# A pose, text, state-space and sparse-attention model on one core: a 42-node operand and two queues in the set-up, and attention units taken in pairs from a copy of the logits in SBUF

## The chip, the core and the metric

The kernel runs on one core of a Trainium2 chip. It is one program for five engines (TensorE or PE, VectorE or DVE, ScalarE or ACT, GpSimd or POOL, SyncE or SP) that meet only through semaphores. The metric is the device time of one execution in microseconds (us); lower is better.

## The reference

Four sequences of 128 frames of 50 joints with 3 coordinates, and four token sequences of 512, are turned into `[4, 640, 128]`. Cut to what matters here:

```python
def _gat(x, src, dst, W, a_s, a_d, bias):          # x [512 frames, 50 joints, channels]
    h = (x @ W).reshape(G, Jn, H, C)               # 4 heads, 148 edges
    es = einsum('gjhc,hc->gjh', h, a_s)[:, src];  ed = einsum('gjhc,hc->gjh', h, a_d)[:, dst]
    ...                                            # softmax over the edges into dst, weighted sum
for W, a_s, a_d, bg, R, g, b in layers:            # channels 3 -> 64 -> 128 -> 64
    x = gelu(layer_norm(_gat(x, ...) + x @ R, g, b))
frames = layer_norm(x.reshape(512, 50 * 64) @ fpW + fpb)
h = concat(frames, conv of one-hot tokens)         # a sum of three gathered rows per token
h = h + state_space_stage(layer_norm(h))           # four layers, 640 steps
x = layer_norm(h);  x = x + depthwise_conv3(x) + pos_b
q, k, v = x @ qkv_w.T + qkv_b                      # 8 heads of 16 channels
idx = top_k(q @ k.T, 16)                           # per query row, 640 keys
h = h + (softmax over those 16 of q @ k.T * scale, times v) @ wo_w.T + wo_b
```

## The kernel before, in words

Three stages follow each other, each a block of its own with a program for each engine: `embed_stage` (0 to about 1350 us), `mamba_stage` (to about 5400 us, untouched by the change) and `ffn_stage` (to the end).

**Embed.** SP issues 5 loads of the token ids once POOL has cleared their tile (`cleared`), then 33 loads of edges and weights with one semaphore, `loaded`, then the frames' coordinates `x0T`, 3 rows by 12800. POOL gathers the token rows by 48 indirect loads. DVE waits for all of `loaded`, then ranks the 148 edges by target (L440 to L456; PE sorts them with one-hot matrices), builds edge masks, and forms for each of the three layers the eight score columns of the weight operand `wc[l]` (L480, L481: weights times `as`, `ad`, summed over a head). `set_dve` (L491) says that this is done. Then come two passes `pb` over pairs of batches. Each pass has three attention layers and the projection of the frames. A layer begins with a projection (`project`, L405): for each of 100 nodes (50 joints of two batches) a matmul with the node's 128 frames as stationary operand and `wc[l]` as moving operand, 136 columns wide in layer 0 (64 of W, 64 of R, 8 scores), with 3 rows in layer 0. Two nodes make a group G (`NG` is 50), ACT copies the first 64 columns of a group to `hbuf` (L321), DVE takes the rest (L529, L531). Then follow edge scores, softmax scans and the products over edges. Buffers `accA` and `accB` take the layers' sums in turn; `x0T` lies in `accB`, so the coordinates of pass 1 are loaded after the last normalisation of pass 0 (`nrm_ready`).

**Attention (`ffn_stage`).** A loop of four batches. A batch has a preparation (L1554 to `vp`: sum, layer norm, transposition, convolution, q, k, v, each step on another engine than the one before) and 40 units c: 5 tiles t of 128 query rows by 8 heads hd. A unit passes through the engines like this:

- PE `logits`: 128x640 of q k into PSUM, `LG[:, k, :]`, k = c % 2 (L1498)
- DVE: the largest 8 of each row (`top1`, L1616), replaced by -3e38 in `cut1` (L1621), the next 8 (`top2`, L1624), replaced in `cut2` (L1629). All four are over 640 elements, each needs the one before; the first two read `LG`
- POOL: `negm`, minus the maximum (L1416)
- ACT: `e_all`, exp of `LG` plus `negm` (L1461), and `e_cut`, exp of `cut2` plus `negm` (L1445)
- POOL `sub`: `prob` is `e_all` minus `e_cut`, which leaves the 16 largest (L1407)
- PE: 5 transposes into `PT` (L1507); ACT: copy to `probT` (L1438); PE: 5 products with `vp`, summed into `Ov` (L1516)
- once in 8 units DVE's `finish_a` (row sums, division), PE's and ACT's output projection of the tile, `finish_b` (residual), SP's store

The order on each engine is written out by hand in one loop over c: in turn c PE does `logits(c+1)`, `transposes(c-2)`, `pv(c-3)`; ACT `exp_cut(c-1)`, `e_all` of c, `probT_copy(c-2)`; POOL `negm` of c, `sub(c-1)`; DVE the four searches of c. `LG` has two halves; `logits(c+1)` waits until unit c-1 has been through both `cut1_ready` and `exp_ready`. The batches are a hardware loop (`Fori`), so a batch's preparation stands behind all of the units of the batch before on every engine.

## Time and profile before

| | us |
|---|---|
| median of 3 runs | 6161.43 |
| range of the runs | 6158.26 to 6162.38 |
| the profiled execution | 6194.43 |
| its span in the trace | 6192.4 |
| busy in the span: DVE, POOL, PE, ACT | 5546.6 (90%), 4510.6 (73%), 3863.3 (62%), 3290.5 (53%) |

The page of the profile is one execution; it took 33 us longer than the median run, and 2.0 us more than its own span. The page's chain of work that ended last is followed back through the last stage only; it names DVE for 7% of the span, issue for 3%, PE for 2%. Its costliest groups of instructions, led by `m_hs` on POOL (2990.4 us) and DVE (2964.0 us), belong to the untouched stage. For the stages of the change the timeline and the windows are read instead. In a window's row the busy times stand in the order PE, PE's weight loads, DVE, ACT, POOL, then PE's granted clock (1.00 is 2.4 GHz, 0.50 is 1.2 GHz), the DMA engines' busy share and GB/s.

### The profile page before, as it was taken

What the parts mean: (1) busy time and instruction counts of PE and PEld (TensorE: products, weight loads), DVE (VectorE), ACT (ScalarE), POOL (GpSimd) and SP (SyncE); (2) the same over time, 40 slices, a digit from 0 to 9 for tenths busy, and PEclk for the clock granted to TensorE, in tenths of its full rate; (3) what the DMA queues carried; (4) which work ended last, traced back from release to release, by engine and by line L of the source; (5) the groups of instructions that cost most, each with busy time, mean ns of one, the idle gap of its engine ahead of it and who ended that gap; (6) DMA issues with size and microseconds to landing.
All of it is one profiled execution on the core that took longest, in us unless ns stands there. A gap on an engine that the chain in (4) does not pass through costs nothing. (4 is left out here: it accounts for less than half of the span.)

```text
span 6192.4 us, 60179 instructions
## 1 busy us (share of the span) xinstructions
PE 3863.3 (62%) x13720; PEld 2225.0 (36%) x13720; DVE 5546.6 (90%) x7803; ACT 3290.5 (53%) x5742; POOL 4510.6 (73%) x3041
## 2 busy tenths in 40 slices
PE   3402432237767677677676776766767766577767
PEld 3202421123334333333333333433333333265556
DVE  3798678839999999999999999999999999787778
ACT  1302232226666666666666666666666665554445
POOL 3303210329999999999999999999999999633334
PEclk9756576659999999999999999999999999888788
DMA  1000000024444444444444444444444444200000
GB/s 28 1 11 1 2 1 11 1 90 173 170 170 168 171 168 170 168 172 169 169 170 168 168 172 169 168 169 168 170 169 171 166 168 169 100 2 2 2 2 2
DMA packets 171471, 694.85 MB, mean 112 GB/s; under 512 B 27969, under 2 KB 34626, under 8 KB 171138
## 3 DMA queue, kind: packets, MB, share of 16 engines
q1 hardware_dynamic: 169608, 688.25, 30.7%
q0 software_dynamic: 1536, 3.14, 0.2%
q14 instruction: 233, 1.91, 0.1%
q8 instruction: 94, 1.54, 0.1%
HBM read 684.77 MB, written 6.55 MB: 112 GB/s over the span
## 5 line engine op out<-in xcount | busy, mean ns | idle before, releaser
L851 POOL TENSOR_TENSOR m_hs<-m_u,m_BC 128x1280 f32<-128x1280 f32 x1024 | 2990.4, 2920 | 76.5 <-DVE m_u L1232 76.5
L1198 DVE TENSOR_TENSOR_SCAN m_hs<-m_PS,m_hs 128x640 f32<-128x640 f32 x2048 | 2964.0, 1476 | 12.6 <-ACT m_PS L908 6.7
L1082 PE MATMUL m_PS<-m_pr,ident 128*128 128x512 f32 (+1 forms) x6144 | 2443.4, 534 | 846.5 <-DVE m_pr L1206 846.1
L1082 PEld LDWEIGHTS m_PS<-m_pr,ident 128*128 128x128 f32 x6144 | 1110.8, 191 | 2079.0 <-DVE m_pr L1206 1077.6
L908 ACT ACTIVATE m_PS<-m_dt,m_A 128x640 f32<-128x640 f32 x2048 | 1612.4, 793 | 430.5 <-DVE m_hs L1198 404.4
L858 POOL TENSOR_TENSOR m_pr<-m_hs,m_BC 128x384 f32<-128x384 f32 x1024 | 1047.5, 1023 | 95.2 <-DVE m_hs L1198 93.4
L1206 DVE TENSOR_TENSOR m_pr<-m_hs,m_PS 128x896 f32<-128x896 f32 x1024 | 1087.4, 1062 | 7.2 <-DVE m_hs L1198 6.9
L292 POOL TENSOR_TENSOR g_prod<-g_hbuf,g_E 128x128 f32<-128x128 f32 x592 | 246.1, 452 | 862.8 <-ACT g_E L344 845.6
L897 ACT COPY m_PS<-m_BC 128x448 f32<-128x448 f32 x1024 | 548.2, 535 | 427.0 <-DVE m_u L1232 83.1
L1416 POOL TENSOR_SCALAR f_negm<-f_top 128x1 f32<-128x1 f32 x160 | 33.5, 209 | 449.4 <-DVE f_top L1616 278.0
L378 PE MATMUL g_TB<-ident,g_nrm 128*128 128x128 f32 x200 | 64.3, 323 | 440.2 <-DVE g_nrm L517 429.2
L1498 PE MATMUL f_LG<-f_kT,f_qh 128*128 128x128 f32 (+1 forms) x640 | 242.2, 508 | 132.4 <-ACT f_e_all L1461 127.3
L346 ACT ACTIVATE g_rstd<-g_rstd 128x100 f32<-128x100 f32 x6 | 1.7, 286 | 582.0 <-DVE g_rstd L621 582.0
L600 DVE TENSOR_TENSOR g_accA<-g_accA,g_prod 128x128 f32 x592 | 223.4, 377 | 52.5 <-issue 23.0
L1407 POOL TENSOR_TENSOR f_prob<-f_e_all,f_e_cut 128x640 f32<-128x640 f32 x160 | 246.4, 1540 | 8.4 <-ACT f_e_cut L1445 8.4
L376 PE MATMUL g_TB<-ident,g_nrm 128*128 128x128 f32 x200 | 45.6, 314 | 321.6 <-DVE g_nrm L517 321.0
L1461 ACT ACTIVATE f_e_all<-f_LG,f_negm 128x640 f32<-128x640 f32 x160 | 126.9, 793 | 173.7 <-DVE f_cut L1621 173.7
L1516 PEld LDWEIGHTS f_O<-f_vp,f_probT 128*128 128x128 f32 x1600 | 218.6, 215 | 0.0
L1516 PE MATMUL f_O<-f_vp,f_probT 128*128 128x17 f32 x1600 | 214.7, 272 | 0.0
L1498 PEld LDWEIGHTS f_LG<-f_kT,f_qh 128*128 128x128 f32 x640 | 122.8, 214 | 239.0 <-issue 123.4
L1120 PE MATMUL m_PS<-m_xT,m_convw 128*128 128x160 f32 x1024 | 179.6, 319 | 43.7 <-DVE m_pr L1206 39.8
L378 PEld LDWEIGHTS g_TB<-ident,g_nrm 128*128 128x128 f32 x200 | 29.3, 147 | 482.4 <-DVE g_nrm L517 270.4
(246 smaller groups left out, 4486.6 us busy)
## 6 DMA issues: line engine op xcount, KB each, us to landing
m_BC<-m_scr SPq DMA_DIRECT2D x1024, 640.0 KB, 3.7
m_scr<-m_CB SPq DMA_DIRECT2D x32, 160.0 KB, 4.3
m_hs<-in_cwr SPq DMA_DIRECT2D x4, 512.0 KB, 3.9
out<-f_res SPq DMA_DIRECT2D x20, 64.0 KB, 1.6
m_inw<-in_in_w SPq DMA_DIRECT2D x4, 256.0 KB, 3.9
m_dtw<-in_dw SPq DMA_DIRECT2D x4, 256.0 KB, 3.6
m_xw<-in_xw SPq DMA_DIRECT2D x8, 64.0 KB, 3.7
m_outw<-in_ow SPq DMA_DIRECT2D x4, 128.0 KB, 3.4
```

The source lines that it names most:

```text
L292: ins = pool.tensor_tensor(slots[:, e % SLOTS[l]].rearrange("p b (h c) -> p b h c", c=C), hb[l][:, :, bass.ds(j, 1), :].rearrange("p b o ( ...
L600: ins = v.tensor_tensor(to, to, slots[:, e % SLOTS[l]], ALU.add)
L851: pool.tensor_tensor(hs[:, g % RH], u[:, p % 2], BC[:, g % UB:g % UB + 1, 0:S].to_broadcast([P, DT, S]), ALU.mult).then_inc(w_ready, 1)
L858: pool.tensor_tensor(pr[:, g % RP, :].rearrange("p (d t) -> p d t", d=DT)[:, :, XD:S], hs[:, g % RH, :, XD:S], BC[:, g % UB:g % UB + 1, S ...
L897: act.copy(C[:, 0:XD], BC[:, g % UB, S:S + XD]).then_inc(c_ready, 1)
L908: act.activation(half[d], dt_[:, p % 2, d], ACT.Exp, scale=A[:, l, d, n:n + 1]).then_inc(da_ready, 1)
L1082: ins = pe.matmul(Y[:, a:e], ident[:], pr[:, g % RP, a:e], start=False, stop=False, skip_group_check=True)
L1198: v.tensor_tensor_scan(hs[:, g % RH, d, :], half[d], hs[:, g % RH, d, :], 0.0, ALU.mult, ALU.add).then_inc(scan_done, 1)
L1206: v.tensor_tensor(pr[:, g % RP, :].rearrange("p (d t) -> p d t", d=DT)[:, :, 0:XD], hs[:, g % RH, :, 0:XD], C[:, 0:XD].unsqueeze(1).to_bro ...
L1407: pool.tensor_tensor(prob[:, k, :], e_all[:, k, :], e_cut[:, k, :], ALU.subtract).then_inc(prob_ready, 1)
L1498: ins = pe.matmul(LG[:, k, a:e], qh[:, hd, t * P:(t + 1) * P], kT[:, a:e], start=True, stop=True)
L1516: ins = pe.matmul(Ov[:, hd, :], probT[:, k, j, :], vp[:, j, hd, :], start=(j == 0), stop=(j == TILES - 1))
```

## The change

**Set-up.** SP issues the 3 edge loads first, before the wait for `cleared`, and behind them 8 loads for layer 0; then the ids and the coordinates. The other 26 loads are issued by ACT. POOL makes its index tiles before it clears. DVE starts the ranking at `edges_loaded`; then come the score columns of layer 0, a mask and the ids (`ids_ready`, on which the gathers wait), then the sorting steps; the score columns of layers 1 and 2 come last, behind `loaded`.

**42-node operand.** In layer 0 the stationary operand is `x0C`, 126 rows: 3 coordinates by 42 nodes, in two overlapping windows (nodes 0 to 41 and 8 to 49). The moving operand is `block0`, 126 rows by 42 blocks of 136 columns, zero but for the rows of the block's own node. ACT makes the 42 blocks (`blocks()`, one activation of 126x136 each, scaled by a column of `mask`) once in the set-up and once more in layer 2 of pass 0. One matmul of 272 columns does a group. Both lie in `accB`; six loads instead of one bring the coordinates, those of pass 1 now after the normalisation in front of layer 2.

**Attention in pairs.** The four batches are written out. A slot n handles units 2n and 2n+1. ACT copies each unit's logits to `lcopy` in SBUF, four deep; the searches and `e_all` read that copy, and `logits` waits for `lcopied` alone. DVE does each of the four steps for both units before the next step. The preparation of batch b+1 (`prepare`, four steps on DVE and PE, three on ACT) stands in slots 20 to 23 of batch b, when the searches are over and PE and ACT still have units to finish.

The core of the diff (the rest are buffer indices, semaphores and the same steps put into functions):

```diff
+wc = [sb(f"wc{l}", [(CROW, P, P)[l], 2 * COUT[l] + 2 * H]) for l in range(3)]
...
-x0T = accB[0:3].rearrange("p (b j) c -> p b j c", b=2)
+N0 = 2 * COUT[0] + 2 * H
+accB_f = accB[0:CROW].rearrange("p j c -> p (j c)")
+block0 = accB_f[:, 0:CH * N0].rearrange("p (j n) -> p j n", n=N0)
+x0C = accB_f[:, CH * N0:CH * N0 + 4 * P].rearrange("p (b k c) -> p b k c", b=2, k=2)
+mask = sb("mask", [CROW, CH])
...
+        for dst, at in ((ei_row[:], T["edges"].unsqueeze(0).to_broadcast([P, 2, NE])),
+                        (ei_col[:, 0, :], T["edgesT"][0:E1, :]), (ei_col[0:E2, 1, :], T["edgesT"][E1:NE, :])):
+            sp.dma_start(dst, at).then_inc(edges_loaded, 16)
+        for dst, at in loads_first():
+            sp.dma_start(dst, at).then_inc(first_loaded, 16)
...
-                sp.wait_ge(nrm_ready, pb * (3 * NG))
-            sp.dma_start(x0T, T["xT"][:, bass.ds(pb * 2, 2)]).then_inc(x_loaded, 16)
+                sp.wait_ge(nrm_ready, (pb * 3 - 1) * NG)
+            for k in range(2):
+                for c in range(3):
+                    sp.dma_start(x0C[CH * c:CH * c + CH, :, k, :],
+                                 T["xT"][c, pb * 2:pb * 2 + 2, CAT[k]:CAT[k] + CH, :].rearrange("b j p -> j b p")
+                                 ).then_inc(x_loaded, 16)
...
+        rest = loads_rest()
+        assert len(rest) == N_REST, len(rest)
+        for dst, at in rest:
+            act.dma_start(dst, at).then_inc(loaded, 16)
+        act.wait_ge(wc0_ready, 1)
+        def blocks():
+            for j in range(CH):
+                act.activation(block0[:, j, :], wc[0][:], ACT.Copy, scale=mask[:, j:j + 1]).then_inc(block_ready, 1)
+        blocks()
+        act.wait_ge(loaded, N_REST * 16)
...
+                if l == 2 and pb + 1 < PB:
+                    act.wait_ge(nrm_ready, (pb * 3 + 2) * NG)
+                    blocks()
...
+                    if l == 0:
+                        k = 0 if 2 * g < CH else 1
+                        at = 2 * g - CAT[k]
+                        pe.matmul(banks(l, G).rearrange("p a n -> p (a n)"), x0C[:, bb, k, :],
+                                  block0[:, at:at + 2, :].rearrange("p a n -> p (a n)"),
+                                  start=True, stop=True).then_inc(proj_ready, 1)
+                        return
...
+        v.wait_ge(edges_loaded, 3 * 16)
         v.wait_ge(iota_ready, 4)
...
+        v.wait_ge(first_loaded, N_FIRST * 16)
+        scores(0, CROW)
+        chain(v.tensor_tensor(mask[:], ident[0:CROW, 0:CH], ident[0:CROW, CH:2 * CH], ALU.add))
+        chain(v.tensor_tensor(mask[:], mask[:], ident[0:CROW, 2 * CH:3 * CH], ALU.add))
+        v.sem_inc(wc0_ready, 1)
+        v.wait_ge(ids_loaded, 5 * 16)
...
+    PAIRS = UNITS // 2
+    PER = HEADS // 2
+    LONG = PAIRS + 5
...
+lcopy = sb("lcopy", [P, 4, S])
...
+            for n in range(PAIRS + 1):
+                if n < PAIRS:
+                    negate(2 * n)
+                    negate(2 * n + 1)
+                if n >= 1:
+                    sub(2 * n - 2)
+                    sub(2 * n - 1)
...
+            def copy_logits(c):
+                act.wait_ge(logits_ready, b * UNITS + (c + 1))
+                if c >= 4:
+                    act.wait_ge(cut1_ready, b * UNITS + (c - 3))
+                    act.wait_ge(exp_ready, b * UNITS + (c - 3))
+                act.copy(lcopy[:, c % 4, :], LG[:, c % 2, 0:S]).then_inc(lcopied, 1)
+            def exp_all(c):
+                act.wait_ge(neg_ready, b * UNITS + (c + 1))
+                if c >= 4:
+                    act.wait_ge(prob_ready, b * UNITS + (c - 3))
+                act.activation(e_all[:, c % 4, :], lcopy[:, c % 4, :], ACT.Exp, bias=negm[:, c % 4:c % 4 + 1]
...
+                for q in range(2):
+                    if 2 <= n < PAIRS + 2:
+                        probT_copy(2 * (n - 2) + q)
+                    if n < PAIRS:
+                        exp_all(2 * n + q)
+                if n + 1 < PAIRS:
+                    copy_logits(2 * n + 2)
+                    copy_logits(2 * n + 3)
+                if n < PAIRS:
+                    exp_cut(2 * n)
+                    exp_cut(2 * n + 1)
+                if b + 1 < B and 0 <= n - PAIRS < 3:
+                    prepare(b + 1, n - PAIRS)
...
-                    pe.wait_ge(cut1_ready, b * UNITS + (c - 1))
-                    pe.wait_ge(exp_ready, b * UNITS + (c - 1))
+                    pe.wait_ge(lcopied, b * UNITS + (c - 1))
...
+            for n in range(LONG):
+                if n >= PER + 3 and (n - PER - 3) % PER == 0:
+                    o_out((n - PER - 3) // PER, 1)
+                old = 2 * (n - 2)
+                if 2 <= n < PAIRS + 2:
+                    transposes(old)
+                    transposes(old + 1)
+                    pv(old)
+                if n + 1 < PAIRS:
+                    logits(2 * n + 2)
+                    logits(2 * n + 3)
+                if 2 <= n < PAIRS + 2:
+                    pv(old + 1)
+                if n >= PER + 2 and (n - PER - 2) % PER == 0:
+                    o_out((n - PER - 2) // PER, 0)
+                if b + 1 < B and 0 <= n - PAIRS < 4:
+                    prepare(b + 1, n - PAIRS)
...
+                two = (2 * n, 2 * n + 1) if n < PAIRS else ()
+                for c in two:
+                    v.wait_ge(lcopied, g0 + (c + 1))
+                    if c >= 4:
+                        v.wait_ge(neg_ready, g0 + (c - 3))
+                    apart(v)
+                    v.max(top1[:, c % 4, :], lcopy[:, c % 4, :]).then_inc(top_ready, 1)
+                if n >= PER + 2 and (n - PER - 2) % PER == 0:
+                    finish_a((n - PER - 2) // PER)
+                if n >= PER + 4 and (n - PER - 4) % PER == 0:
+                    finish_b((n - PER - 4) // PER)
+                for c in two:
+                    v.wait_ge(top_ready, g0 + (c + 1))
                     if c >= 2:
-                        v.wait_ge(neg_ready, g0 + (c - 1))
+                        v.wait_ge(cut2_ready, g0 + (c - 1))
                     apart(v)
-                    v.max(top1[:, k, :], LG[:, k, 0:S]).then_inc(top_ready, 1)
-                    v.wait_ge(top_ready, g0 + (c + 1))
-                    if c >= 1:
-                        v.wait_ge(cut2_ready, g0 + c)
-                    apart(v)
-                    v.match_replace(cut1[:], top1[:, k, :], LG[:, k, 0:S], CUT).then_inc(cut1_ready, 1)
+                    v.match_replace(cut1[:, c % 2, :], top1[:, c % 4, :], lcopy[:, c % 4, :], CUT).then_inc(cut1_ready, 1)
+                for c in two:
                     v.wait_ge(cut1_ready, g0 + (c + 1))
                     apart(v)
-                    v.max(top2[:, k, :], cut1[:]).then_inc(top2_ready, 1)
+                    v.max(top2[:, c % 2, :], cut1[:, c % 2, :]).then_inc(top2_ready, 1)
+                for c in two:
                     v.wait_ge(top2_ready, g0 + (c + 1))
                     if c >= 2:
                         v.wait_ge(expcut_ready, g0 + (c - 1))
                     apart(v)
-                    v.match_replace(cut2[:, k, :], top2[:, k, :], cut1[:], CUT).then_inc(cut2_ready, 1)
-                if c >= HEADS + 2 and (c - HEADS - 2) % HEADS == 0:
-                    finish_a((c - HEADS - 2) // HEADS)
-                if c >= HEADS + 4 and (c - HEADS - 4) % HEADS == 0:
-                    finish_b((c - HEADS - 4) // HEADS)
+                    v.match_replace(cut2[:, c % 2, :], top2[:, c % 2, :], cut1[:, c % 2, :], CUT).then_inc(cut2_ready, 1)
+                if b + 1 < B and 0 <= n - PAIRS < 4:
+                    prepare(b + 1, n - PAIRS)
```

ACT in the steady stretch, before: one unit to a turn (`f_` names the stage; `e_cut`, `e_all` and the copy to `probT`).

```order
L1438 COPY f_probT<-f_PT 128x640 [waits f_pv_done,f_probT_ready]
L1445 ACTIVATE f_e_cut<-f_cut,f_negm 128x640 [waits f_prob_ready,f_cut2_ready]
L1457 REGISTER_ALU
L1461 ACTIVATE f_e_all<-f_LG,f_negm 128x640 [waits f_prob_ready,f_cut1_ready,f_neg_ready]
L1438 COPY f_probT<-f_PT 128x640 [waits f_pv_done,f_probT_ready]
L1445 ACTIVATE f_e_cut<-f_cut,f_negm 128x640 [waits f_prob_ready,f_cut2_ready]
L1457 REGISTER_ALU
```

The same place now: the copies of the logits are new, and everything comes twice (two rows of `probT` and `e_all` alternate).

```order
L1530 COPY f_lcopy<-f_LG 128x640 [waits f_exp_ready,f_cut1_ready,f_logits_ready] x2
L1522 ACTIVATE f_e_cut<-f_cut,f_negm 128x640 [waits f_prob_ready,f_cut2_ready] x2
L1515 COPY f_probT<-f_PT 128x640 [waits f_pv_done,f_probT_ready]
L1536 ACTIVATE f_e_all<-f_lcopy,f_negm 128x640 [waits f_prob_ready,f_neg_ready]
L1515 COPY f_probT<-f_PT 128x640 [waits f_pv_done,f_probT_ready]
L1536 ACTIVATE f_e_all<-f_lcopy,f_negm 128x640 [waits f_prob_ready,f_neg_ready]
L1530 COPY f_lcopy<-f_LG 128x640 [waits f_exp_ready,f_cut1_ready,f_logits_ready] x2
```

`e_all` no longer waits for `cut1_ready`, and a unit's copy of the logits stands ahead of the `e_cut` of the pair before.

PE in the same stretch, before, one turn:

```order
L1498 MATMUL f_LG<-f_kT,f_qh 128x512 [waits f_exp_ready,f_cut1_ready]
L1498 MATMUL f_LG<-f_kT,f_qh 128x128
L1507 MATMUL f_PT<-ident,f_prob 128x128 [waits f_probT_copied,f_prob_ready]
L1507 MATMUL f_PT<-ident,f_prob 128x128 x4
L1516 MATMUL f_O<-f_vp,f_probT 128x17 [waits f_probT_copied]
L1516 MATMUL f_O<-f_vp,f_probT 128x17 x4
```

Now, one slot (transposes of two units, one PV, logits of two units, the other PV):

```order
L1610 MATMUL f_PT<-ident,f_prob 128x128 [waits f_probT_copied,f_prob_ready]
L1610 MATMUL f_PT<-ident,f_prob 128x128 x4
L1610 MATMUL f_PT<-ident,f_prob 128x128 [waits f_probT_copied,f_prob_ready]
L1610 MATMUL f_PT<-ident,f_prob 128x128 x4
L1619 MATMUL f_O<-f_vp,f_probT 128x17 [waits f_probT_copied]
L1619 MATMUL f_O<-f_vp,f_probT 128x17 x4
L1599 MATMUL f_LG<-f_kT,f_qh 128x512 [waits f_lcopied]
L1599 MATMUL f_LG<-f_kT,f_qh 128x128
L1599 MATMUL f_LG<-f_kT,f_qh 128x512 [waits f_lcopied]
L1599 MATMUL f_LG<-f_kT,f_qh 128x128
L1619 MATMUL f_O<-f_vp,f_probT 128x17 [waits f_probT_copied]
L1619 MATMUL f_O<-f_vp,f_probT 128x17 x4
```

The logits come behind the transposes and a PV whose waits are on `prob` and `probT`, and wait for ACT's copy instead of DVE and the exponential.

SP's queue at the start, now (before, the ids came first and `g_accB<-in_xT` behind all 38 others):

```order
L268 DMA g_E<-in_edges 128x296
L268 DMA g_ei_col<-in_edgesT 128x2
L268 DMA g_ei_col<-in_edgesT 20x2
L270 DMA g_wc<-in_W 42x64
...
L270 DMA g_M<-in_ad 128x64
L272 DMA g_ids<-in_ids 128x16
...
L276 DMA g_ids<-in_ids 1x4x3
L282 DMA g_accB<-in_xT 42x2x128 x6
L286 DMA g_hbuf<-in_fpW 128x25x128
L282 DMA g_accB<-in_xT 42x2x128 x6
```

The edges lead, the coordinates follow the ids, and the second set waits for `g_nrm_ready` of an earlier layer.

## Rows read from the trace of the kernel before

**Rows 1.** windows: from:to length, then busy us (x instructions) of PE, PEld, DVE, ACT, POOL; clock.

```profile
5420.00:6192.00 772.00, 572.86 (x3182) 454.96 (x3180) 600.51 (x1134) 372.65 (x517) 278.21 (x323) 0.84 0.01 2
```

**Rows 2.** timeline of the set-up: start us, us, engine, line, operation, [idle before it].

```profile
9.91 0.45 SPq L248 DMA_DIRECT2D g_E<-in_edges  x1
11.07 0.17 DVE L436 TENSOR_SCALAR g_ids<-g_ids 128x16 int32<-128x16 int32 x1 [11.07 <-DMA g_ids<-in_ids]
...
30.06 0.24 DVE L440 CAST g_F<-g_E 128x148 f32<-128x148 int32 x1 [18.74 <-DMA g_fnb<-in_fnb]
...
76.79 0.14 DVE L491 MEMSET g_dif<- 128x100 f32 x1 [4.10 <-remote]
77.46 45.70 PE L405 MATMUL g_PJ<-g_wc,g_accB 3*128 3x136 f32 x200 [40.76 <-DVE g_dif L491]
```

**Rows 3.** windows in the set-up and in two projections of the pose stage.

```profile
30.00:39.60 9.60, 3.23 (x8) 2.00 (x8) 5.52 (x25) 0.00 (x0) 7.47 (x8) 1.00 0.23 55
39.60:76.80 37.20, 0.00 (x0) 0.00 (x0) 7.83 (x29) 0.00 (x0) 27.08 (x28) 1.00 0.19 49
460.00:470.00 10.00, 8.60 (x53) 7.19 (x54) 6.53 (x32) 6.29 (x17) 0.00 (x0) 0.88 0.01 2
665.00:700.00 35.00, 35.00 (x156) 35.00 (x156) 14.34 (x78) 10.22 (x39) 0.00 (x0) 0.50 0.00 1
```

**Rows 4.** timeline, PE: a layer-1 projection matmul group, and the second layer-0 projection.

```profile
463.07 0.63 PE L405 MATMUL g_PJ<-g_wc,g_xTs 128*128 128x136 f32 x4
...
657.74 45.69 PE L405 MATMUL g_PJ<-g_wc,g_accB 3*128 3x136 f32 x200 [4.49 <-DMA g_accB<-in_xT]
```

**Rows 5.** timeline, ACT with two pointer operands, five instructions.

```profile
5395.20 2.03 ACT L1047 ACTIVATE x_tok<-x_tok,m_nmr,m_rstd 128x128 f32<-128x128 f32 x5
```

**Rows 6.** timeline of one attention unit in its steady stretch, all engines.

```profile
5459.13 0.82 DVE L1616 MAX8 f_top<-f_LG 128x8 f32<-128x640 f32 x1
5459.25 0.84 ACT L1445 ACTIVATE f_e_cut<-f_cut,f_negm 128x640 f32<-128x640 f32 x1 [0.61 <-DVE f_cut L1629]
5459.35 0.71 PE L1507 MATMUL f_PT<-ident,f_prob 128*128 128x128 f32 x5
5459.90 1.19 PE L1516 MATMUL f_O<-f_vp,f_probT 128*128 128x17 f32 x10
...
5461.10 0.79 ACT L1461 ACTIVATE f_e_all<-f_LG,f_negm 128x640 f32<-128x640 f32 x1 [1.02 <-DVE f_cut L1621]
5461.17 0.83 DVE L1624 MAX8 f_top<-f_cut 128x8 f32<-128x640 f32 x1
5461.80 0.68 ACT L1438 COPY f_probT<-f_PT 128x640 f32<-128x640 f32 x1
5462.04 1.32 PE L1498 MATMUL f_LG<-f_kT,f_qh 128*128 128x512 f32 x4 [0.96 <-ACT f_e_all L1461]
5462.25 0.81 DVE L1629 MATCH_REPLACE8 f_cut<-f_top,f_cut 128x640 f32<-128x640 f32 x1
5462.97 0.82 DVE L1616 MAX8 f_top<-f_LG 128x8 f32<-128x640 f32 x1
```

**Rows 7.** windows in attention batch 0: the whole, 32 us of it, 4 us of it.

```profile
5432.00:5592.00 160.00, 130.10 (x742) 104.31 (x741) 136.79 (x252) 89.85 (x124) 68.07 (x80) 0.87 0.01 3
5452.00:5484.00 32.00, 23.99 (x162) 19.43 (x160) 27.66 (x52) 18.21 (x26) 13.67 (x16) 1.00 0.01 1
5488.00:5492.00 4.00, 4.00 (x18) 3.48 (x17) 3.45 (x8) 2.21 (x4) 1.76 (x3) 0.50 0.00 0
```

**Rows 8.** timeline, DVE and PE, from the last search of batch 0 to the first of batch 1.

```profile
5589.09 0.81 DVE L1629 MATCH_REPLACE8 f_cut<-f_top,f_cut 128x640 f32<-128x640 f32 x1
...
5603.77 0.83 DVE L1554 TENSOR_TENSOR f_h<-h_tok,x_tok 128x640 f32 x1 [3.25 <-issue]
...
5608.43 1.33 PE L1474 MATMUL f_LG<-ident,f_xn 128*128 128x128 f32 x5 [8.23 <-DVE f_xn L1570]
...
5628.94 0.83 DVE L1616 MAX8 f_top<-f_LG 128x8 f32<-128x640 f32 x1 [2.78 <-PE f_LG L1498]
```

331 lines of the change are left out of this document (172 added, 159 removed).

## The prediction

> **What bounds the kernel now.** I read the page for the shares of each engine, the windows for each stage, then the timeline around the three places of the change. Every rebuilt place is on the path: the stages follow each other, and nothing of one stands under the next. In the attention stage DVE is busy 600.51 of 772 us, PE 572.86, ACT 372.65 [rows 1]. A unit shows why DVE is not simply full: `top1` starts at 5459.13 and the next unit's at 5462.97, 3.84 us for four operations of 0.81 to 0.83. The last one starts 1.08 behind the operation it depends on (5461.17 to 5462.25), and the next unit's first, which depends on no DVE result, 0.72 behind it (5462.97 less 5462.25) [rows 6]. So 3.84 is 0.72 and three dependent steps of (3.84 − 0.72)/3 = 1.04. It is a chain, not a full engine. In the set-up DVE starts the edges at 30.06, after 18.74 us of waiting for the last of all loads, and PE's first projection waits 40.76 for DVE's last set-up operation [rows 2]. Layer 0's projection is PE alone: 45.70 and 45.69 us [rows 2, 4], busy 35.00 of 35.00 [rows 3].
>
> **Set-up.** The three edge loads no longer wait for the clearing or the ids. Before, one edge load took 0.45 to issue at 9.91 and the last ids landed at 11.07 [rows 2]; DVE then waited to 30.06. With the edges first, I take the start at about 6.4, 23.7 earlier. How fast DVE then goes is the unknown: 25 operations from 30.0 to 39.6 (9.60/25 = 0.38 each, PE's sort included), but 29 operations from 39.6 to 76.8 (37.20/29 = 1.28 each), of which 7.83 us are busy [rows 3]. The gathers run under both, so they alone don't explain it, and the excess, 29 × (1.28 − 0.38) = 26 us, is near the 33 us by which the profiled execution exceeds the median run. I read this as mostly the profiled execution's own. At the fast pace the median kernel starts its projection at 77.5 − 26 = 51.4; after the change 54 operations of 0.38 end at 6.4 + 20.5 = 26.9, but ACT's 42 block activations start only behind layer 0's scores and the mask, at about 15, and at 0.41 each (five pointer activations in 2.03) [rows 5] end at 32. That gives 51.4 − 32 = 19, or 16 if the blocks begin 3 us later. At the profiled pace it is 23.7 plus the four layer-0 score operations, which move to where PE's sort is waited for anyway (4 × 1.28): 29. I take **−20**, nearer the first since the sum goes to the median. ACT's 26 loads take time in which it had nothing to do, and SP's six coordinate loads instead of one land long before 32. The ids are ready a few us later, hence the gathers too; their rows are needed only in the mamba stage. The second `blocks()` (42 × 0.41 = 17 us) lies on ACT while DVE and POOL aggregate layer 2: nothing; if that cover is gone, up to 17.
>
> **Layer 0.** 45.70 us for 50 groups is 0.914 a group of two nodes, at the lower clock: the granted clock is 0.50 from 665 to 700 while PE is busy all the time with a 3-row operand. Streams of 128 rows fare otherwise: in 460 to 470 PE is busy 8.60 of 10.00 and the clock is 0.88 on average [rows 3], and a group of the same width then takes 0.63 with its latency [rows 4]. 126 rows are near 128. At 2.4 GHz a group is 0.457 and a pass 22.9; ACT (10.22 us for 39 copies, 0.26) and DVE (14.34/39 = 0.37 a group) [rows 3] keep up. Pass 0: −22.9 and +3 for the start at the lower clock, **−19.9**. Pass 1: −22.9, and the 4.49 of waiting for the coordinates [rows 4] goes, since they are loaded a layer earlier: **−27.4**. A page of the Trainium skill ("TensorE: Matmul & The Clock Gate", its Part 1) lets the gate go by how busy PE has been and says nothing of rows; by that the fully busy 3-row stream should have had the full clock, and what is denied to it would be denied to 126 rows too. The row shows 0.50 at 35.00 of 35.00, against the page.
>
> **Attention, steady.** In pairs no DVE operation depends on the one in front, so DVE needs 8 × 0.72 to 0.82, with 0.77 taken 6.16 a pair against 7.68 now [rows 6]. Then another cycle is longer, round ACT and PE. By their order, from the second `e_cut`: 0.75 (0.84 less the 0.09 by which ACT's next overlaps, as `e_all` of 0.79 is followed after 0.70), `probT` copy 0.68 and 0.15 to PE, one set of transposes 0.55, PV 1.09, first logits 1.16 (1.32 less the end that the next covers), second logits 1.32 and 0.05, ACT's copy of them 0.59, first `e_cut` 0.75 [rows 6]. The sum is 0.75 + 0.83 + 0.55 + 1.09 + 1.16 + 1.37 + 0.59 + 0.75 = **7.09 a pair**. The copy of 128x640 from PSUM is priced as `probT`, the same shape. ACT's own work is 2 × (0.84 + 0.79 + 0.68 + 0.68) = 5.98, POOL's 13.67/32 × 7.68 = 3.3 [rows 7]: both fit. Gain 0.59 × 80 pairs = **−47**. The "VectorE: DVE Perf Modes" page of the Trainium skill (section "The DRAIN you can't avoid") says that the next DVE operation can't issue before the pipe is empty, semaphore or not; by it the pairing would give DVE nothing. The rows show 0.72 against 1.04, so only the dependent ones pay in full.
>
> **Attention, clock.** PE was off the path, now it is on it. In batch 0 the mean clock is 0.87: a quarter of 160 us at half clock. Before, that was free: DVE is busy 3.45 of 4 us at 0.50, and 27.66 of 32 (the same share) at 1.00 [rows 7]. Now each us at half clock costs: PE's work is 23.99/32 × 7.68 = 5.76 a pair, 11.5 at half, 4.4 more than 7.09. The bounds are 0 (PE works 0.81 of the time instead of 0.75) and all 42 us a batch (42 × (1 − 7.09/11.5) × 4 = 64). I take six us a batch, **+24**.
>
> **Batch boundaries.** From the last search (5589.09 + 0.81) to the next batch's first (5628.94) are 39.0 us: 13.9 to the first preparation operation at 5603.77, 4.7 to PE's first at 5608.43, 20.5 more [rows 8]. The 20.5 stay. The 13.9 go, but PE's first preparation stands behind transposes and PV of four units at half clock, 4 × 2 × (0.55 + 1.09) = 13, so 15 or so remain: 35.6, bounds 30 and 37. Three boundaries: **−10**. The first copy and a tail in pairs: **+3**.
>
> **Sum:** −20 − 19.9 − 27.4 − 47 + 24 − 10 + 3 = −97.3, so 6161.4 − 97.3 = **6064**. A profiled execution, from 6194.4, would be 6088 to 6097. The forecast's own range, from the bounds above (set-up −29 to −16, clock 0 to +64), is 6031 to 6108.
>
> **Rivals.**
> - *The rows are not what holds the clock.* Layer 0 stays at 0.914 a group: 19.9 + 22.9 back, 6107. It is what the page's rule amounts to. For: one case of 3 rows. Against: the two windows [rows 3]. Chance 0.10.
> - *DVE keeps 3.84 a unit*, by the drain rule or since `neg_ready` and `cut2_ready` arrive late. The clock costs nothing then: 6161.4 − 67.3 − 7 = 6087. Against it the 0.72. Chance 0.07.
> - *ACT and PE overlap better than my cycle*: DVE binds at 6.16, (7.09 − 6.16) × 80 = 75 less: 5989. For: four-deep buffers. Against: every link is in the order. Chance 0.10.
> - *The early start meets the gathers*: if operations under them cost 1.28 in each run, layer 0's DVE take is slowed too, +17: 6081. Chance 0.08.
> - *Slower: PE's clock falls.* Pairs bunch PE's work with a gap behind each ACT copy and `e_cut`; if the clock halves for many pairs, each costs 4.4. With half of the 80, 176 less the 24 counted: 6216. It turns into a loss from (97.3 + 24)/4.4 = 28 pairs, a third. Before, a quarter of the time was at half clock. Against: the clock rose within 460 to 470 while PE was busy 8.60 of 10 [rows 3], and a PE at half clock is busier. Chance 0.04.
>
> **The numbers.** The forecast keeps 0.61. Range **5985 to 6110**: it takes in four of the rivals' points and leaves out the slower one and half of the best. 0.2% (12 us) is about what a measurement of this kernel can tell from no change. Faster by more: all but the slower rival and the two first together, 0.94; the same 0.02; slower 0.04.
>
> **What would show it.** DVE's first edge operation near 6, the first projection at 32 to 48; layer 0 about 23 to 26 us with clock 1.00; no wait before the second; in attention DVE waiting on ACT's `lcopy` or ACT on PE, a pair in 7.1; boundaries of 36. Wrong would be: layer 0 at 45 us, DVE spaced 1.04 with two units in turn, or a mean clock in attention under 0.8.

## The result and the profile after

| | before | changed |
|---|---|---|
| median of 8 runs | 6161.03 | 6130.24 |
| range | 6158.26 to 6168.02 | 6118.59 to 6156.98 |
| profiled execution (span) | 6194.43 (6192.4) | 6127.35 (6125.6) |

The ratio is 0.9954, interval 0.9938 to 0.997: 31 us faster, a third of the 97 forecast and outside the range. The runs also spread wider, over 38 us instead of 10. The ratios leave out an execution that is more than 1.5% above the fastest of its kernel (one of the runs below, of e2).

The page after: busy time of each engine, and the chain of work that ended last. Before, the chain named DVE first with 7%; now PE, with ACT behind.

```profile
PE 3875.6 (63%) x13520; PEld 2193.6 (36%) x13520; DVE 5510.1 (90%) x7805; ACT 3413.9 (56%) x5986; POOL 4515.1 (74%) x3041
PE 8%; ACT 2%; issue 2%; DVE 1%; POOL 0%; ACTq 0%; DVEq 0%; POOLq 0%
```

The window of the attention stage of the changed kernel (columns as ahead of the prediction). It runs at a mean clock of 0.77, below the 0.8 that the prediction named as a sign of being wrong; before it was 0.84 [rows 1].

```profile
5306.00:6125.00 819.00, 633.96 (x3192) 486.42 (x3192) 570.81 (x1156) 468.20 (x680) 284.46 (x324) 0.77 0.01 2
```

Where the time went is read from the starts of the stages. The attention stage's first DVE operation stood at 5407.13 before and stands here (timeline, DVE):

```profile
5305.84 0.83 DVE L1666 TENSOR_TENSOR f_h<-h_tok,x_tok 128x640 f32<-128x640 f32 x1 [7.88 <-POOL f_tap L1463]
```

The first instruction of the middle stage starts at 1160.5 here and started at 1253.6 before (not near 1350, as the text ahead of the prediction has it). So set-up and pose stage gained 93 us in this pair of profiled executions; 8 more, to 101.3, lie in the middle stage, whose code is the same. The attention stage took 6125.6 − 5305.8 = 819.8 us where it had taken 6192.4 − 5407.1 = 785.3: **34.5 us more**, where 30 less were forecast. Of the 93 us, some 28 are the slow stretch of the profiled execution of before: in the profile of e2 below, which has the old set-up and pose stage, the middle stage starts at 1225.9.

The timeline of the set-up and of the second layer-0 projection, after. It answers to [rows 2, 4].

```profile
7.47 0.24 DVE L498 CAST g_F<-g_E 128x148 f32<-128x148 int32 x1 [7.47 <-DMA g_ei_col<-in_edgesT]
...
17.47 1.28 ACT L343 ACT_TABLE_LOAD   x1 [17.47 <-issue]
18.77 12.65 ACT L343 ACTIVATE g_accB<-g_wc,g_mask 126x136 f32<-126x136 f32 x42
...
26.75 0.14 DVE L554 MEMSET g_dif<- 128x100 f32 x1
31.56 25.73 PE L449 MATMUL g_PJ<-g_accB 126*128 126x272 f32 x100 [17.75 <-ACT g_accB L343]
...
587.68 23.18 PE L449 MATMUL g_PJ<-g_accB 126*128 126x272 f32 x100
```

DVE starts at 7.47 instead of 30.06 and is through its last set-up operation at 26.75; ACT's 42 blocks end at 31.42, and PE starts at 31.56, within 0.5 us of the forecast 32. That closeness is luck: the mask for the blocks is ready at 14.74, as forecast, but ACT issues its own 26 loads until 17.44 and then loads a table for 1.28, so the blocks begin at 18.77 and not at 15; and they take 0.30 each, not 0.41. The two errors, +3.8 and −4.6 us, cancel. The passes take 25.73 and 23.18 us (forecast 25.9 and 22.9), and the second waits for nothing.

In attention two kinds of slot alternate. PE at the full clock, from one first PV to the next, 5482.11 to 5489.03, is 6.92 us (forecast 7.09):

```profile
5482.11 1.19 PE L1619 MATMUL f_O<-f_vp,f_probT 128*128 128x17 f32 x10
5483.15 2.41 PE L1599 MATMUL f_LG<-f_kT,f_qh 128*128 128x512 f32 x8
...
5486.43 0.74 PE L1610 MATMUL f_PT<-ident,f_prob 128*128 128x128 f32 x5
5488.46 0.74 PE L1610 MATMUL f_PT<-ident,f_prob 128*128 128x128 f32 x5 [1.28 <-ACT f_probT L1515]
5489.03 1.19 PE L1619 MATMUL f_O<-f_vp,f_probT 128*128 128x17 f32 x10
```

And PE in another part of the same batch, 5369.58 to 5379.77, 10.19 us:

```profile
5368.48 1.30 PE L1610 MATMUL f_PT<-ident,f_prob 128*128 128x128 f32 x5 [1.28 <-ACT f_probT L1515]
5369.58 2.16 PE L1619 MATMUL f_O<-f_vp,f_probT 128*128 128x17 f32 x10
5371.57 4.21 PE L1599 MATMUL f_LG<-f_kT,f_qh 128*128 128x512 f32 x8
5375.61 1.19 PE L1619 MATMUL f_O<-f_vp,f_probT 128*128 128x17 f32 x10
5376.65 0.74 PE L1610 MATMUL f_PT<-ident,f_prob 128*128 128x128 f32 x5
5378.68 1.30 PE L1610 MATMUL f_PT<-ident,f_prob 128*128 128x128 f32 x5 [1.29 <-ACT f_probT L1515]
5379.77 2.16 PE L1619 MATMUL f_O<-f_vp,f_probT 128*128 128x17 f32 x10
```

Read the second list by its durations. The PV at 5375.61 and the first transposes at 5376.65 have the full-clock lengths 1.19 and 0.74. Then PE waits 1.29 us, and the second transposes take 1.30, the next PV 2.16, the logits 4.21 for two. By these lengths the clock fell in the wait, came back during the logits, and fell in the next wait. The granted clock says so too, in windows in front of the wait and behind it:

```profile
5376.00:5378.00 2.00, 1.39 (x13) 1.15 (x12) 1.32 (x3) 2.00 (x4) 0.49 (x3) 1.00 0.00 0
5379.00:5385.00 6.00, 6.00 (x21) 4.45 (x20) 3.13 (x7) 2.38 (x4) 1.96 (x2) 0.50 0.01 4
```

The wait is the same in both kinds of slot: `PT` is one buffer, so the second set of transposes waits until ACT has copied the first, and ACT comes to that only behind both `e_cut` (timeline, ACT, at the wait of the full-clock slot):

```profile
5486.18 1.55 ACT L1522 ACTIVATE f_e_cut<-f_cut,f_negm 128x640 f32<-128x640 f32 x2
5487.63 0.68 ACT L1515 COPY f_probT<-f_PT 128x640 f32<-128x640 f32 x1
```

The first transposes are through at 5487.17, the copy runs from 5487.63 to 5488.31, PE goes on at 5488.46. Within batch 0 (waits of PE: us in total, times, longest; and the window):

```profile
PE f_PT L1610 <- ACT f_probT L1515: 23.1, 18, 3.3
```

```profile
5333.00:5499.00 166.00, 133.00 (x704) 101.38 (x702) 127.34 (x253) 109.07 (x159) 66.28 (x78) 0.82 0.01 2
```

The spacing of DVE's first search from slot to slot tells how often: of 76 spacings inside the four batches 22 are 9.4 us or more. From first to last search the batches take 165.8, 158.3, 171.1 and 166.0 us, before 157.6, 158.0, 157.7 and 157.6. Of this the clock stood at its lower level for 59, 45, 75 and 59 us (twice the missing share of the granted clock, times the length), before for 38, 32, 25 and 24. PE's idle time does not go with it: 33 us in each of the four batches, and 30 to 36 before, there mostly in waits of 0.95 for `e_all`, in front of a unit's logits.

A batch boundary, DVE and PE, answering to [rows 8]: the last search ends at 5498.83, the preparation starts at once, and PE comes to it 14.5 us later, at 5513.37.

```profile
5498.02 0.81 DVE L1756 MATCH_REPLACE8 f_cut<-f_top,f_cut 128x640 f32<-128x640 f32 x1
5498.94 0.94 DVE L1666 TENSOR_TENSOR f_h<-h_tok,x_tok 128x640 f32<-128x640 f32 x1
...
5513.37 1.31 PE L1576 MATMUL f_LG<-ident,f_xn 128*128 128x128 f32 x5
```

The next first search comes at 5535.06, 36.2 us behind the last (forecast 35.6; before 39.0).

### The profile page after: what moved, and what is told of

Its sections match the earlier page's. It is cut to its first block and busy times, and to the rows that moved or that the text cites. A ratio compares the mean times of both kernels' runs of the same rounds, so it can differ in the third digit from the quotient of the medians.

```text
span 6125.6 us, 59162 instructions
## 1 busy us (share of the span) xinstructions
PE 3875.6 (63%) x13520; PEld 2193.6 (36%) x13520; DVE 5510.1 (90%) x7805; ACT 3413.9 (56%) x5986; POOL 4515.1 (74%) x3041
## 5 line engine op out<-in xcount | busy, mean ns | idle before, releaser
L1736 DVE MAX8 f_top<-f_lcopy 128x8 f32<-128x640 f32 x160 | 131.5, 826 | 164.8 <-ACT f_lcopy L1530 160.5
L1599 PE MATMUL f_LG<-f_kT,f_qh 128*128 128x128 f32 (+1 forms) x640 | 259.8, 564 | 12.7 <-ACT f_lcopy L1530 8.0
L1619 PEld LDWEIGHTS f_O<-f_vp,f_probT 128*128 128x128 f32 x1600 | 241.8, 235 | 0.0
L1619 PE MATMUL f_O<-f_vp,f_probT 128*128 128x17 f32 x1600 | 236.7, 288 | 0.0
L1530 ACT COPY f_lcopy<-f_LG 128x640 f32<-128x640 f32 x160 | 109.9, 692 | 210.6 <-PE f_LG L1599 210.6
L1610 PE MATMUL f_PT<-ident,f_prob 128*128 128x128 f32 x800 | 140.2, 315 | 111.1 <-ACT f_probT L1515 98.7
```

Of the source, the lines that this page charges most:

```text
L1599: ins = pe.matmul(LG[:, k, a:e], qh[:, hd, t * P:(t + 1) * P], kT[:, a:e], start=True, stop=True)
L1619: ins = pe.matmul(Ov[:, hd, :], probT[:, k, j, :], vp[:, j, hd, :], start=(j == 0), stop=(j == TILES - 1))
```

## The experiments

Twelve kernels and three more for what they left open. Each was compared with the kernel before on its own chip, where that has a median of 6163 to 6165 unless another number stands beside. Where two experiments of different chips are set against each other, the difference of the medians and that of the ratios can differ by some us.

**e1, e2: the two halves apart.** e1 has the new set-up and pose stage with the old attention, e2 the reverse.

> The pose stage and set-up of the change, the attention stage of before. Theory (the pose part gave what was forecast, about -65 us against the median of before, and attention gave 34 us back): 6094 to 6098. Rival (the profiled set-up of before was slow only in its own execution, and the pose part is worth less in a plain run): 6110 to 6130.

> The pose stage and set-up of before, the attention stage of the change. Theory (attention in pairs is slower since PE falls to half clock for many slots): 6185 to 6205, slots of 6.9 us at full clock and of 10.2 at half. Rival (attention is no slower by itself and is upset by what runs in front): 6115 to 6160. Its profile is also a second look at the old set-up: if its projection starts near 77 us again, the slow stretch under the gathers belongs to the kernel; if near 50, to one execution.

e1: 6093.15, ratio 0.9885 (0.9868 to 0.9901), before 6164.25: −71, 1 us beyond the expected range. e2: 6203.59, ratio 1.0065 (1.0038 to 1.0092): +39, with runs from 6183 to 6320. Both as the theory had it: the new attention stage loses half of what the rest gains. The old set-up, seen a second time in e2 (timeline):

```profile
30.48 0.24 DVE L440 CAST g_F<-g_E 128x148 f32<-128x148 int32 x1 [19.26 <-DMA g_fnb<-in_fnb]
...
48.61 0.14 DVE L491 MEMSET g_dif<- 128x100 f32 x1
...
48.81 45.69 PE L405 MATMUL g_PJ<-g_wc,g_accB 3*128 3x136 f32 x200 [11.91 <-DVE g_dif L491]
```

DVE's 54 operations take 18.1 us here, and the projection starts at 48.81, not at 77.46. So the slow stretch doesn't belong to each run of before, and without it the set-up is worth 48.8 − 31.6 = 17 us. From this profile to that of the changed kernel the start of the middle stage moves from 1225.9 to 1160.5, by 65 us (forecast 67.3).

**e3: a filler in the wait.**

```diff
                             transposes(old)
+                            if n + 1 < PAIRS:
+                                pe.wait_ge(lcopied, b * UNITS + (2 * n + 1))
+                                for _ in range(5):
+                                    pe.transpose(LG[:, 0, 640:768], ident[:], ident[:])
                             transposes(old + 1)
```

> The changed kernel with five useless 128x128 transposes into an unused part of PSUM in each slot, where PE waits 1.28 us between the two sets of transposes: more PE work, no less of anything. Theory (the short idle makes the clock fall, and the clock makes the slot 10.2 instead of 6.9): the slots at half clock become rare, 40 to 90 us faster than the changed kernel, 6040 to 6090. Rival (PE is simply too full, or the order is at fault): the added 0.55 to 1.1 us a slot makes it 10 to 60 us slower.

6060.4, ratio 0.9841 (0.9819 to 0.9863). **Useless work made the kernel 70 us faster** than the changed one. PE's timeline in a slot (the filler is L1645), and the window of batch 0:

```profile
5368.51 0.74 PE L1610 MATMUL f_PT<-ident,f_prob 128*128 128x128 f32 x5
5369.09 0.71 PE L1645 MATMUL f_LG<-ident 128*128 128x128 f32 x5
5370.53 0.74 PE L1610 MATMUL f_PT<-ident,f_prob 128*128 128x128 f32 x5 [0.74 <-ACT f_probT L1515]
5331.00:5480.00 149.00, 126.30 (x786) 100.76 (x784) 126.94 (x251) 108.80 (x159) 65.91 (x78) 0.91 0.01 2
```

The filler takes the place of part of the wait, 0.74 is left, and in this slot everything behind it keeps its full-clock length. The clock over the batch is 0.91 instead of 0.82, and the batch 148.9 us long instead of 165.8. Over the four batches the time at the lower clock is 88 us instead of 238, and 7 spacings of 76 are 9.4 us or more instead of 22. A slot at the full clock stays at 6.9 us, so it is the clock that gained. The order of the work is unchanged; PE waits for the copy of unit 2n one step earlier, a wait that `logits(2 * n + 2)` has anyhow.

**e6: the same filler where PE doesn't wait.** The five transposes stand in front of `logits(2 * n + 2)` instead.

> The five useless transposes of the filler run, but put in front of the first logits of a slot, where PE does not wait; the 1.28 us wait between the two sets of transposes stays. Theory (it is the wait at that place that lets the clock fall): no gain, 6130 to 6190, since the work lies on the cycle. Rival (any added work keeps the clock up, wherever it stands): 6060 to 6100.

6180.3, ratio 1.0023 (1.0014 to 1.0033), before 6164.36: 50 us slower than the changed kernel (43 by the ratios). PE's timeline and window:

```profile
5407.60 0.74 PE L1610 MATMUL f_PT<-ident,f_prob 128*128 128x128 f32 x5
5409.63 1.23 PE L1610 MATMUL f_PT<-ident,f_prob 128*128 128x128 f32 x5 [1.28 <-ACT f_probT L1515]
5341.00:5520.00 179.00, 145.80 (x786) 113.60 (x784) 126.90 (x251) 108.80 (x158) 66.15 (x78) 0.81 0.01 2
```

As much added work as in e3, but the wait of 1.28 stands, the second transposes behind it take 1.23 instead of 0.74, and the clock is 0.81. So added work by itself doesn't keep the clock up; work that takes the place of idle time does. PE is idle 33 us in this batch, as in the changed kernel, and 23 us in e3's: whether the length of the single wait counts or the idle time in all, the two runs don't separate.

**e4: logits in the wait.**

```diff
                         if 2 <= n < PAIRS + 2:
                             transposes(old)
+                        if n + 1 < PAIRS:
+                            logits(2 * n + 2)
+                        if 2 <= n < PAIRS + 2:
                             transposes(old + 1)
                             pv(old)
                         if n + 1 < PAIRS:
-                            logits(2 * n + 2)
                             logits(2 * n + 3)
```

> The changed kernel, PE's order in a slot: transposes, logits of unit 2n+2, transposes, PV, logits of 2n+3, PV. The same work, with one logits in the place of the 1.28 us wait. Theory (the idle between the transposes is what costs clock and 1.3 us of the cycle): slots of 6.1 to 6.5 and few at half clock, 60 to 110 us faster than the changed kernel, 6020 to 6070. Rival (the clock falls by the total of PE's work in a slot, which is the same): the slots at half clock stay, within 25 us of the changed kernel.

6010.54, ratio 0.9748 (0.9731 to 0.9766): 120 us faster than the changed kernel, 10 us beyond the expected range.

```profile
5381.11 0.74 PE L1610 MATMUL f_PT<-ident,f_prob 128*128 128x128 f32 x5
5381.69 1.25 PE L1599 MATMUL f_LG<-f_kT,f_qh 128*128 128x512 f32 x4
5383.14 0.74 PE L1610 MATMUL f_PT<-ident,f_prob 128*128 128x128 f32 x5 [0.20 <-ACT f_probT L1515]
5340.00:5472.00 132.00, 116.17 (x697) 91.17 (x695) 124.47 (x251) 108.01 (x159) 66.09 (x78) 0.90 0.01 3
```

The wait is 0.20. Spacings are 6.1 to 6.6 us in most slots, and 6.1 is DVE's own 8 × 0.76: DVE binds now. Both effects are in this number, the shorter cycle (6.9 to 6.1, about 0.8 × 80 = 64 us) and the clock.

**e5: the copy alone.** The new pose stage, attention in the old order, but ACT copies the logits and all readers use the copy.

> Set-up and pose stage of the change; attention in the old order, unit by unit, but ACT copies each unit's logits to SBUF (two deep) and the searches, e_all and PE's release go by the copy. Theory (the copy by itself gives nothing: DVE's chain of three dependent steps stays, 3.84 us a unit): within 10 us of the kernel with the old attention (6093). Rival (reading PSUM or waiting for PE is part of the 3.84): 3.5 us a unit or less, over 40 us faster than 6093.

6101.18, ratio 0.9899 (0.9882 to 0.9915), against e1's 6093: nothing gained, 8 us lost (7 from the first search to the end, in the traces). Spacings are mostly the old 7.7 for two units, each batch's first takes 8.6 instead of 7.6, and a batch boundary 40 instead of 39. The copy buys nothing without the pairs.

**e11: pairs without the copy.** The searches and `e_all` read `LG`, `logits` waits for `cut1_ready` and `exp_ready` again, and `e_all` for its own unit's `cut1_ready`.

> The changed kernel without ACT's copy of the logits: searches and e_all read PSUM, PE's logits wait for cut1 and e_all of the unit two before, all in pairs as in the change. Theory (the cycle through ACT and PE is what binds, and the copy lies on it twice with 0.6 us, while DVE reads PSUM as fast): DVE or nearly DVE binds at 6.1 to 6.8 a pair at full clock, 30 to 90 us faster than the changed kernel, 6040 to 6100. Rival (the copy is what lets PE run ahead; without it DVE waits for logits): 7.4 us a pair or more, 6130 or slower.

6047.35 (6027.09 to 6080.99), ratio 0.9821 (0.978 to 0.9861): 83 us *faster* than with the copy. The window of its second batch, 135.6 us from first to last search:

```profile
5533.00:5669.00 136.00, 111.96 (x697) 85.68 (x696) 126.90 (x252) 85.69 (x119) 66.35 (x78) 0.94 0.01 2
```

DVE reads the logits in PSUM as fast as the copy in SBUF (`top1` takes 0.82 to 0.83 us from either); the same pairing gives spacings of mostly 6.1 to 7.1. ACT is busy 85.69 us, in the changed kernel 109.07. The copy isn't what makes the pairs possible, and it lies on their cycle. Without it PE's wait between the transposes is also shorter, 0.87 instead of 1.28, so the gain has two parts that this run doesn't separate. The first batch of this execution took 162.0 us, with slots of 11 and more and 70 us at the lower clock, where the second has 16. PE's waits between the transposes are the same in both (15.7 us in 18 waits), and PE's idle time too (24 us): with the shorter wait the falls are rare in three batches of four, but it doesn't rule them out. e4's order without the copy was not tried.

**e8, e9: what lets layer 0 run at the full clock.** e8 keeps 126 rows and goes back to two matmuls of 136 columns; e9 keeps the one matmul of 272 and takes 3 rows of both operands.

> The changed kernel, but layer 0 with two matmuls of 136 columns for a group of two nodes instead of one of 272, the same 126-row operand loaded twice. Theory (the rows give the clock, not the width): 0.46 a group, layer 0 within 3 us of 25.7, the whole within noise of 6130. Rival (half the weight loads is what halved the time): 40 to 46 us a pass, 6160 to 6170.

> The set-up and pose stage of the change with the old attention, but layer 0's matmul of 272 columns gets only the first 3 of the 126 rows of both operands (it leaves out all nodes but one of a window, and two coordinates' rows). Time alone counts. Theory (few rows keep the clock at its lower level however busy PE is): 0.91 a group, 45 us a pass, clock 0.50 in the second pass, 6135 to 6142. Rival (the width of 272 or one weight load a group gave the clock): 0.46 a group and 6091 to 6098 as with 126 rows.

e8: in the trace its two layer-0 projections take 26.28 and 23.43 us, in the changed kernel 25.73 and 23.18, at a granted clock of 1.00 (592 to 610 us). Its median, 6153.78 (6130.7 to 6204.3; ratio 0.9997, 0.9971 to 1.0023), is 24 us above the changed kernel's and so misses "within noise of 6130". Layer 0 doesn't explain that in the one execution that was profiled, the fastest, at 6130.7; what the slower ones did was not seen. Its attention stage is the changed one, and two of its batches show how far the clock moves a batch (windows of the first and the second):

```profile
5338.00:5486.00 148.00, 114.83 (x702) 88.53 (x700) 126.86 (x252) 108.89 (x159) 66.15 (x78) 0.93 0.01 2
5522.00:5693.00 171.00, 138.54 (x692) 105.01 (x691) 127.08 (x251) 108.06 (x157) 65.27 (x78) 0.78 0.01 2
```

The first took 148.3 us with 21 at the lower clock and no spacing of 9.4 or more, the second 171.1 us with 75. PE's idle time is 33 us in both, and its wait between the transposes is 1.28 in most slots of both.

e9, which leaves out 123 of the 126 rows and so does only a small part of the sum: 6136.3, ratio 0.9954 (0.9938 to 0.997). Its second pass (timeline and window):

```profile
607.76 43.72 PE L449 MATMUL g_PJ<-g_accB 3*128 3x272 f32 x100
615.00:650.00 35.00, 35.00 (x79) 25.30 (x78) 14.16 (x77) 10.34 (x39) 0.00 (x0) 0.50 0.00 0
```

43.72 us, 0.87 a group, at a clock of 0.50 with PE busy 35.00 of 35.00. With 126 rows the same instruction stream took 23.18. With e8 and the kernel before, each width was run with few and with many rows: the rows give the clock, not the width and not the number of weight loads. Against e1 e9's median is 6136 − 6093 = 43 us higher, and its two passes are 40 us longer in the traces (45.67 and 43.72 against 25.80 and 23.18); the prediction had 42.8. The page "TensorE: Matmul & The Clock Gate" of the Trainium skill (Part 1) lets the clock go by how busy PE has been; here the measurement decides against it.

**e10: one queue.** ACT's 26 loads go to SP behind the coordinates.

> The set-up and pose stage of the change with the old attention, but the 26 remaining loads are issued by SP behind the coordinates instead of by ACT. Theory (ACT's blocks hold the first projection at 31.8 us, and the scores of layers 1 and 2 would now wait for loads that land near 33): the first projection at 36 to 39, 4 to 7 us slower than 6093. Rival (the second queue gives nothing): within 1.5 us of 6093.

6094.09, ratio 0.9886 (0.987 to 0.9903), against e1's 6093.15. Timeline:

```profile
11.66 12.65 ACT L342 ACTIVATE g_accB<-g_wc,g_mask 126x136 f32<-126x136 f32 x42 [7.68 <-DVEq L518]
...
29.83 0.29 DVE L491 TENSOR_TENSOR g_M<-g_wc,g_M 128x128 f32<-128x128 f32 x1 [9.70 <-DMA g_fnb<-in_fnb]
...
33.96 24.59 PE L448 MATMUL g_PJ<-g_accB 126*128 126x272 f32 x100 [20.48 <-DVE g_dif L553]
```

The median is that of the rival, within 1.5 us of e1, and the expected 4 to 7 us didn't come. ACT's blocks, free of the loads, begin at 11.66 and end at 24.3, 7 us earlier than in the changed kernel; but the last loads hold DVE's second scores until 29.83, and the projection starts at 33.96 instead of 31.8. So the second queue only decides whom PE waits for, ACT with its blocks or DVE with its scores, and gives no time that these runs can tell. What remains as the source of the set-up's gain is that the edges come first and that DVE no longer waits for all loads.

**e7, e12: further along the same line.** e7 is e4 with the next batch's preparation one slot earlier; e12 adds the following on PE:

```diff
-                        if n >= PER + 3 and (n - PER - 3) % PER == 0:
-                            o_out((n - PER - 3) // PER, 1)
                         old = 2 * (n - 2)
...
                             transposes(old + 1)
                             pv(old)
+                        if n >= PER + 3 and (n - PER - 3) % PER == 0:
+                            o_out((n - PER - 3) // PER, 1)
```

> The kernel with logits in the wait between the transposes, and the next batch's preparation one slot earlier on DVE, ACT and PE (slots 19 to 22 instead of 20 to 23). Theory (PE's leftover transposes and PV at half clock gate the boundary of 38.6 us): each boundary 4 to 7 us shorter, 5990 to 6000. Rival (the boundary is the preparation's own chain and DVE's finish steps): within 3 us of 6010 for the three boundaries.

> The kernel of e7, with the second half of a tile's output projection (once in four slots) moved on PE from a slot's start to behind its first PV, so that PE does not wait there for ACT's copy of oT (1.32 us in e4's trace). Theory (PE's waits inside a slot are what make single slots 7.5 to 9 us and cost clock): slots of 6.1 to 6.6 throughout, 15 to 30 us faster than e7's 5992, 5962 to 5977. Rival (those slots are long from DVE's own finish steps or from the clock whatever the wait): within 8 us of 5992.

e7: 5992.27, ratio 0.9729 (0.971 to 0.9748), boundaries of 33.9 to 35.2 instead of 38.6 to 39.0, 12 us for the three. e12: 6016.73 where the kernel before takes 6193.05, ratio 0.9716 (0.9699 to 0.9732): by the ratio no gain over e7, and outside both ranges of its expectation. From the first search to the end it took 633.4 us, 25 less than e7, but the first pass's layer-0 projection, which starts at 31.56 as ever, took 70.68 instead of the 25.2 of e7. DVE in layer 0 of that execution, and POOL's last gather:

```profile
66.36 0.29 DVE L592 TENSOR_TENSOR g_accA<-g_PJ,g_bgb 128x128 f32<-128x128 f32 x1 [5.22 <-issue]
66.57 0.17 DVE L594 COPY g_esd<-g_PJ 128x16 f32<-128x16 f32 x1
71.95 0.29 DVE L592 TENSOR_TENSOR g_accA<-g_PJ,g_bgb 128x128 f32<-128x128 f32 x1 [5.22 <-issue]
...
80.95 0.99 POOL L302 DMA_INDIRECT g_after<-in_table,g_ids  x1 [0.30 <-issue]
```

Two DVE operations, then 5.22 us in which DVE waits for nothing the profile shows; so it goes on to 86, and from there on, with the last gather done at 81.9, a group of two follows 0.3 to 0.9 behind the one in front again. The stretch looks like the slow stretch of [rows 3], on a chip where the kernel before takes 29 us more (7 runs, 6185 to 6207).

**e13 to e15: what stayed open.** e7 and e12 again on one chip, and e12 with the gathers held behind layer 0 (`pool.wait_ge(acc_ready, NG)` in front of them).

> e7 once more, beside the next two on one chip. Theory (e12's move is worth its 25 us in the attention stage, and the set-up's slow stretch in e12's execution hid it): e7's attention stage at 658 us from the first search to the end, and e12's repeat 15 to 30 us faster than this one. Rival: within 8 us of it.

> e12 once more on the same chip as e13. Theory: 15 to 30 us faster than e13, 5962 to 5977 where the kernel before takes 6161 to 6165; where that takes some 6190, its profile shows DVE operations far apart under the gathers, and it is near 6015. Rival (the output step's place gives nothing): within 8 us of e13.

> e12's kernel, with POOL's 48 gathers held until layer 0 of the first pass is taken over (57 us instead of 17 us; POOL's first other work comes near 130 us). Theory (the gathers can hold up DVE's instructions on some chips, 46 us in e12's execution, and layer 0 is where that costs most): on a chip where the kernel before takes 6190, 20 to 45 us faster than e14 with layer 0 back at 25 us; on one where it takes 6163, within 5 us of e14. Rival (the slow stretch has nothing to do with the gathers): the stretch stays where it was, or no change on either kind of chip.

e13: 5988.52, ratio 0.971 (0.9694 to 0.9726). e14: **5970.87**, ratio 0.9685 (0.9668 to 0.9701): as expected, the output step's place gains, by 18 us, and this is the fastest kernel of the study, 194 us below before (6164.72 on this chip). e15: 6009.34, ratio 0.9747 (0.973 to 0.9763), 38 us slower than e14, against the expectation of no change on a chip like this one. POOL's timeline:

```profile
121.49 1.00 POOL L303 DMA_INDIRECT g_after<-in_table,g_ids  x1 [0.30 <-issue]
122.50 39.97 POOL L325 TENSOR_TENSOR g_prod<-g_hbuf,g_E 128x128 f32<-128x128 f32 x96
```

I had taken POOL's first product for some 130 us, but that is when it starts in e12's slow execution (129.1). In e14 it starts at 84.3, where the gathers had just ended (at 81.3), and here they end at 122.5. So the gathers are close to the path of the changed kernel, and holding them back costs what it moves them by. Whether they are what holds DVE up on the other kind of chip stays open: this chip didn't show the stretch with the gathers in either place, and no run had the held-back gathers on a chip that does.

## Why the prediction was wrong

**Right, by its own steps.** The start of the first projection was forecast at 32 and came at 31.56, by luck: the loads on ACT, priced at nothing, hold the blocks back by 3.8 us, and shorter blocks give 4.6 back. The old start, without the slow stretch, was forecast at 51.4 and is 48.81 in e2: −17 where −20 was taken. Layer 0 −20.0 and −22.5 against −19.9 and −22.9, and the 4.49 of waiting went. The sum of set-up and pose stage, −67.3, measured −71 in e1 and −65 in the traces. The reading of the slow stretch of [rows 3] as no part of the median run fits the medians of before on every chip of the study but one; as "the profiled execution's own" it was too simple, since on e12's chip the kernel before takes 29 us more as a median of 7 runs. The rival of the rows was tested by e9 and fell.

**Right in attention:** a slot at the full clock is 6.92 (7.09 forecast), DVE's operations in pairs come 0.76 apart (0.77), a boundary is 36.2 (35.6). The rival by which DVE can't overlap fell with that.

**Wrong: the term "clock, +24".** The four batches from first to last search take 661.2 us. At 7.09 a pair they would be 567, so the term was 94, four times what I took and above its bound of 64. The step that failed is the one that took the half-clock time over from before: 42 us a batch as the most there could be, with the reason that PE would work more of the time. Measured were 59, 45, 75 and 59 us a batch, 238 in all; before it was 119. The price of such a time was right: at the prediction's 1 − 7.09/11.5 = 0.38 a us the 238 are 91 us, near the 94. The share of time that PE works was no guide to the clock: 0.79 to 0.81 now, 0.77 to 0.81 before, and at the same idle time a batch the lower clock came twice as long. The clock is not a given of the stage. The order of the change puts a wait of 1.28 us into most slots, and what runs behind that wait is on the cycle, at half speed where the clock has fallen; e6 has more work and the same clock, e3 has the wait half filled and is 70 us faster. Why the same idle time costs more clock as waits of 1.28 than it did as waits of 0.95 stays open. I had added the length of each link of the cycle and not asked where PE stands idle in it: between the two sets of transposes, for the rest of ACT's `e_cut` pair, the `probT` copy of 0.68, and the way there and back. All of that could be read from the order in the diff and the lengths in [rows 6].

The rest of the attention stage is small. The gain of 47 was reckoned from 7.68 a pair, but the batches of before take 631.0 us, 7.89 a pair, since their spacings with a tile's finishing steps in them are mostly 7.9 to 8.4; so from 631.0 to 567 are 64, and 94 less 64 is the 30 by which the batches got longer. The boundaries gave 4 of the 10 (two of them 36.2, one 39.7), and the part in front of the first search and behind the last is 8 us longer, not 3. That is 30 − 4 + 8, the 34 us more of the stage.

**The slower rival** named the mechanism, "Pairs bunch PE's work with a gap behind each ACT copy and `e_cut`", with the price of 4.4 a pair (measured 10.19 − 6.92 = 3.3) and put the turn at 28 pairs. Some 22 slots fell, at 3.3 us 73 of the 94; the rest is in other slots, where the clock was low for a shorter time. For the attention stage alone that was enough to turn the gain into a loss; the pose stage's gain covered it. I had given it 0.04 and only the extreme; what came was the middle of it, over a quarter of the slots, which the sum had no term for. *ACT and PE overlap better than my cycle* did not happen by itself, but one line of order (e4) made it so.

## What to carry to other kernels

When TensorE is on the cycle of a loop, list where it stands idle within one turn, not only how busy it is: behind a wait of 1.3 us once in 7 the work ran at half speed in a quarter of the turns here, and moving other work into that place, even useless work, was worth more than the whole change. Before a copy to SBUF is added so that readers let go of PSUM, try the new order without it. And time two halves of a change apart: here one half gained 71 us and the other lost 39, and the sum looked like a small success.
